# Both scores ahead of the product block in each attention step, with one third of the maximum products between them

## The chip, the cores and the metric

One Trainium2 chip, one core of it. The time is that of the device for one execution, in microseconds. The kernel before took 2652.84 us, the median of three runs (2650.61 to 2661.35).

## What is computed

The reference is one pre-norm transformer layer in fp32 on x of shape (2, 2048, 512): a causal attention with 16 heads of 32, and a feed-forward part with 8 experts of which each token uses 2, plus a shared one. The part that matters here:

```
scores = einsum('bhqd,bhkd->bhqk', q, k) / sqrt(32)
scores = where(causal, scores, -inf)
attn   = softmax(scores, axis=-1)
out    = einsum('bhqk,bhkd->bhqd', attn, v)
```

So each score is exponentiated less the maximum of its row, the row's sum divides at the end, and keys behind the query are masked.

## The kernel before

The phases follow one another: projections, attention, output projection with the shared expert, routing, experts, combination. Only `phase_attention` (L507 to L982) is touched.

Its unit of work is one group of 4 heads (8 groups over the two batches) and one chunk of 512 queries, q = 0 to 3, so 32 units. A unit goes through its key tiles of 128 keys in the order of `ORDER[q]`; the tiles from 4q on lie on the diagonal and need the mask. Each tile makes two steps, p = 0 and p = 1 (two heads each), 640 steps in all, and since every unit has an even number of steps p = 0 is an even step and p = 1 an odd one.

The row maxima of a unit are found one unit or so ahead, by a second, transposed product of q and k: a stream of 1280 "max" items and one "turn" per unit. `attention_plan` (L420) deals this stream out to the steps, `upto`, by costs that it gives the items and the room it sees in each step: mostly 3 items in odd steps, 0 to 2 in even ones. `item_shares` (L540) cuts the items of a step in three: with one item it falls into the last third, with two into the last two, with three one goes into each.

In a step, TensorE does:

- `score(n, 0)` and `score(n, 1)` (L907, the matmul at L918), each into the next of three banks `b_st` (NST = 3), so each waits for the exponential of the third score before it (L913). The second score of step n waits for the first exponential of step n-1.
- `item(i)` (L880): a maximum product (L897) into the next of three banks `b_mx`, which waits until VectorE has read the bank used three items before (L885); or the turn, four transposes (L904) of a finished unit's maxima.
- in odd steps `values` (L921), eight recorded matmuls for the two steps that lie 3 and 2 back; in even steps `count_ones` (L936), the row sums of the tile two back, if that tile is not in `POOL_TILES` (those tiles GpSimd adds up, L657, and `finish` adds them at a unit's end).

VectorE reads each maximum product (L781, on the diagonal L778) and masks the two scores of a diagonal step in their banks with one instruction (L802) or two (L806), waiting for the second score (L799). ScalarE makes the two exponentials of a step (L840) out of the banks into one of eight buffers `b_pt`; in a masked step both wait for the mask (L837). A turn's rows are copied by ScalarE (L846) ahead of the exponentials of the step whose items hold the turn (L865 to L868), and SyncE then moves them into `b_q`. All orders are written out; nothing is rearranged at run time.

The tables that place the tiles and the row sums:

```
ORDER = ((0, 1, 2, 3), (0, 1, 4, 2, 5, 3, 6, 7), (0, 1, 2, 8, 3, 4, 9, 5, 6, 10, 7, 11),
         (0, 1, 2, 12, 3, 4, 5, 13, 6, 7, 8, 14, 9, 10, 11, 15))
ONES_TILES = ((0, 1, 2, 3), (2, 6, 7), (2, 9, 6, 10, 11), (2, 4, 13, 8, 14, 15))
```

Of the kernel before, what the change touches and what calls it, by code (L numbers as in the profile page):

```python
# [46 lines left out]
def f32(ap):  # L47

    return ap.bitcast(F32)
# [457 lines left out]
def phase_attention(nc, x, w, scratch, ahead):  # L507
# [32 lines left out]
    def item_shares(n):  # L540

        here, there = upto[n - 1] if n else start, upto[n]
        return [here + (there - here) * k // 3 for k in range(4)]
# [20 lines left out]
    def key_slot(it, j):  # L564

        return (NQ * it + j) % KRING

    def unit_ending(n, offset):

        for u in range(NU):  # L570
            if first_step[u + 1] + (offset[units[u][1]] if isinstance(offset, tuple) else offset) == n:
                return u
        return None

    with ExitStack() as ctx:
# [52 lines left out]
        with nc.Block() as block:  # L628
# [140 lines left out]
            @block.vector  # L769
            def _(v):  # L770
                def partial_max(i):
                    _, u, t, h, c = stream[i]
                    q = units[u][1]
                    w = min(CH, (TPC * q + t + 1) * P - c * CH)
                    v.wait_ge(s_item, i + 1)
                    part = mpart[u % 2][:, t, h, c:c + 1]
                    if c == q:
                        v.tensor_tensor_reduce(unread[i % NMX][:, 0:w], mxb[i % NMX][:, 0:w], later[:, CH - w:], 1.0, -3e38,  # L778
                                               ALU.add, ALU.max, part).then_inc(s_red, 1)
                    else:  # L780
                        v.tensor_reduce(part, mxb[i % NMX][:, 0:w], AX.X, ALU.max).then_inc(s_red, 1)  # L781
                    if (t, h, c) == (TPC - 1, HG - 1, q):
                        v.wait_ge(s_red, maxes_before[i + 1])
                        v.tensor_reduce(mt[u % 2][:, :, 0:MROW + 1:DH], mpart[u % 2][:, :, :, 0:q + 1],
                                        AX.X, ALU.max, negate=True).then_inc(s_mcol, 1)

                v.memset(f32(kb[MROW:MROW + 1]), 1.0).then_inc(s_set, 1)
                for n in range(2):
                    v.memset(mt[n][:], 0.0).then_inc(s_set, 1)  # L789
                v.wait_ge(s_set, NSET)  # L790
                v.wait_ge(s_cst, NCST)
                for i in range(start):
                    if stream[i][0] == "max":
                        partial_max(i)
                def mask(n):
                    u, q, kt, p = steps[n]
                    d = kt - TPC * q
                    b0 = 2 * n % NST
                    v.wait_ge(s_st, 2 * n + 2)  # L799
                    if b0 + 1 < NST:  # L800
                        block = stb[:, b0:b0 + 2, d * P:(d + 1) * P]
                        v.tensor_tensor(block, block, sooner[:].unsqueeze(1).to_broadcast([P, 2, P]), ALU.add).then_inc(s_msk, 1)  # L802
                    else:
                        for b in (b0, 0):
                            block = stb[:, b, d * P:(d + 1) * P]
                            ins = v.tensor_tensor(block, block, sooner[:], ALU.add)  # L806
                        ins.then_inc(s_msk, 1)

                for n in range(NS):
                    here, _, some, there = item_shares(n)  # L810
                    for i in range(here, some):
                        if stream[i][0] == "max":
                            partial_max(i)
                    if steps[n][2] >= TPC * steps[n][1]:
                        mask(n)
                    for i in range(some, there):
                        if stream[i][0] == "max":
                            partial_max(i)
                    if n == first_step[NQ * NG - 2]:
                        v.wait_ge(s_sum, 16)  # L820
                        v.reciprocal(rsum[:], sums[:]).then_inc(s_rec, 1)
# [57 lines left out]
            def _(pe):  # L879
                def item(i):  # L880
                    what = stream[i]
                    bank = mxb[i % NMX]
                    if i >= NMX:
                        if stream[i - NMX][0] == "max":
                            pe.wait_ge(s_red, maxes_before[i - NMX + 1])  # L885
                        else:
                            pe.wait_ge(s_turn, stream[i - NMX][1] + 1)
                    if what[0] == "max":
                        _, u, t, h, c = what
                        it, q = units[u]  # L890
                        w = min(CH, (TPC * q + t + 1) * P - c * CH)
                        if (t, h, c) == (0, 0, 0):
                            pe.wait_ge(s_q[q], 48 * (it + 1))
                        if (t, h) == (0, 0) and c == q:
                            pe.wait_ge(s_k[c][it % 2], 48 * (it // 2 + 1))
                        at = key_slot(it, c) * CH
                        ins = pe.matmul(bank[:, 0:max(w, 2 * P)], qb[0:KR, h, q * CH + t * P:q * CH + (t + 1) * P],  # L897
                                        kb[0:KR, h, at:at + max(w, 2 * P)], start=True, stop=True)
                        ins.then_inc(s_item, 1)
                    else:  # L900
                        u = what[1]
                        pe.wait_ge(s_mcol, u + 1)
                        for t in range(TPC):
                            ins = pe.transpose(bank[0:MROW + 1, t * P:(t + 1) * P], mt[u % 2][:, t, :], ident[:])  # L904
                        ins.then_inc(s_item, 1)

                def score(n, j):  # L907
                    u, q, kt, p = steps[n]
                    it = units[u][0]
                    d = kt - TPC * q  # L910
                    lo = min(max(d, 0) * P, 2 * P)
                    if 2 * n + j >= NST:
                        pe.wait_ge(s_exp, 2 * n + j - NST + 1)  # L913
                    if n == first_step[u] and j == 0:
                        pe.wait_ge(s_row[q], 16 * (it + 1))
                    at = key_slot(it, kt // TPC) * CH + kt % TPC * P
                    h = 2 * p + j
                    pe.matmul(stb[:, (2 * n + j) % NST, lo:], kb[:, h, at:at + P],  # L918
                              qb[:, h, q * CH + lo:(q + 1) * CH], start=True, stop=True).then_inc(s_st, 1)
# [16 lines left out]
                def count_ones(m):  # L936
                    u, q, kt, _ = steps[2 * m]
                    if kt in POOL_TILES[q]:
                        return
                    lo = max(kt - TPC * q, 0) * P  # L940
                    begin = ONES_TILES[q][0]
                    if kt == begin and u:
                        pe.wait_ge(s_sev, u)
                    for h in range(HG):
                        ins = pe.matmul(sb[h * DH:(h + 1) * DH, lo:], ones[:],  # L945
                                        pt[(2 * m + h // 2) % NPB][:, h % 2, lo:],
                                        start=(kt == begin), stop=(kt == ORDER[q][-1] and not POOL_TILES[q]))
                    ins.then_inc(s_one, 1)
# [13 lines left out]
                for n in range(NS):  # L962
                    here, *some = item_shares(n)
                    score(n, 0)
                    for i in range(here, some[0]):
                        item(i)
                    if n % 2 == 0 and n >= 4:
                        count_ones((n - 4) // 2)
                    if n % 2 and n >= 3:
                        values((n - 3) // 2)  # L970
                    for i in range(some[0], some[1]):
                        item(i)
                    score(n, 1)
                    for i in range(some[1], some[2]):
                        item(i)
                    done = unit_ending(n, FINISH)
                    if done is not None and done in summed:
                        finish(done)
# [940 lines left out]
```

## Time and profile before

| | |
|---|---|
| median of three runs | 2652.84 us |
| profiled execution, its own time | 2644.25 us |
| its span | 2642.6 us |
| TensorE busy | 2319.7 us, 88% |
| VectorE busy | 1559.6 us, 59% |
| ScalarE busy | 1045.4 us, 40% |
| GpSimd busy | 1002.3 us, 38% |

PE is TensorE's matmuls and PEld its weight loads, which overlap them; DVE is VectorE, ACT ScalarE, POOL GpSimd. Matmuls are pipelined: a row's length is that of one matmul from start to end, and the next can start before it ends. Idle time in brackets is that of the engine just before the row, with what released it.

### The profile page before, as it was taken

What the parts mean: (1) busy time and instruction counts of PE and PEld (TensorE: products, weight loads), DVE (VectorE), ACT (ScalarE), POOL (GpSimd) and SP (SyncE); (2) the same over time, 40 slices, a digit from 0 to 9 for tenths busy, and PEclk for the clock granted to TensorE, in tenths of its full rate; (3) what the DMA queues carried; (4) which work ended last, traced back from release to release, by engine and by line L of the source; (5) the groups of instructions that cost most, each with busy time, mean ns of one, the idle gap of its engine ahead of it and who ended that gap; (6) DMA issues with size and microseconds to landing.
All of it is one profiled execution on the core that took longest, in us unless ns stands there. A gap on an engine that the chain in (4) does not pass through costs nothing. (4 is left out here: it accounts for less than half of the span.)

```text
span 2642.6 us, 34529 instructions
## 1 busy us (share of the span) xinstructions
PE 2319.7 (88%) x12088; PEld 1469.9 (56%) x12088; DVE 1559.6 (59%) x3219; ACT 1045.4 (40%) x1928; POOL 1002.3 (38%) x592
## 2 busy tenths in 40 slices
PE   5996699999999999999999599998499999999940
PEld 5775344444444444444443377776477777777730
DVE  3664686767777767767673444443645545555535
ACT  2332155555555555555556412121033333333300
POOL 0000055575655566665657613130221212111036
PEclk8998599999999999999999799999599999999975
DMA  3766511313131403323210234331245454545349
GB/s 114 272 243 224 113 33 49 81 35 93 36 81 33 97 24 93 82 57 73 49 51 23 70 114 143 113 126 50 85 146 175 144 179 139 180 136 174 96 172 368
DMA packets 178740, 301.72 MB, mean 114 GB/s; under 512 B 23616, under 2 KB 65728, under 8 KB 178624
## 3 DMA queue, kind: packets, MB, share of 16 engines
q1 hardware_dynamic: 159360, 242.54, 30.3%
q0 software_dynamic: 14656, 49.29, 6.0%
q10 hardware_dynamic: 4608, 8.39, 0.8%
q8 instruction: 66, 1.08, 0.2%
q14 instruction: 50, 0.41, 0.1%
HBM read 199.65 MB, written 100.27 MB: 113 GB/s over the span
## 5 line engine op out<-in xcount | busy, mean ns | idle before, releaser
L840 ACT ACTIVATE b_pt<-b_st 128x512 f32<-128x512 f32 (+3 forms) x1280 | 612.6, 535 | 484.4 <-DVE b_st L802 205.4
L657 POOL TENSOR_TENSOR b_acc<-b_acc,b_pt 128x1024 f32<-128x1024 f32 (+1 forms) x256 | 593.0, 2346 | 214.1 <-ACT b_pt L840 213.7
L781 DVE TENSOR_REDUCE b_mpart<-b_mx 128x1 f32<-128x512 f32 x768 | 512.2, 686 | 195.6 <-PE b_mx L897 193.0
L918 PE MATMUL b_st<-b_q,b_k 97*128 97x512 f32 (+2 forms) x1280 | 495.1, 400 | 74.2 <-ACT b_pt L840 54.7
L897 PE MATMUL b_mx<-b_k,b_q 96*128 96x512 f32 (+2 forms) x1280 | 506.6, 411 | 29.9 <-DVE b_mt L789 25.9
L897 PEld LDWEIGHTS b_mx<-b_k,b_q 96*128 96x128 f32 x1280 | 247.0, 194 | 284.9 <-DVE b_mpart L781 154.0
L918 PEld LDWEIGHTS b_st<-b_q,b_k 97*128 97x128 f32 x1280 | 241.0, 190 | 279.3 <-ACT b_pt L840 240.6
L931 PE MATMUL b_ob<-b_pt,b_v 128*32 128x512 f32 (+3 forms) x2560 | 303.0, 545 | 1.1 <-ACT b_pt L840 1.1
L778 DVE CUSTOM_DVE_ANT_0 b_unread<-b_mx,b_later 128x384 bf16<-128x384 f32 (+3 forms) x512 | 245.0, 485 | 87.7 <-PE b_mx L897 87.3
L657 POOL TENSOR_TENSOR b_acc<-b_pt 128x1024 f32<-128x1024 f32 x48 | 113.4, 2378 | 294.7 <-ACT b_pt L840 294.7
L61 PE MATMUL e_fb<-e_xh,e_w_guh 128*128 128x512 f32 (+1 forms) x552 | 219.6, 398 | 1.5 <-DVE e_xl L1738 1.5
L63 PE MATMUL e_fb<-e_xl,e_w_guh 128*128 128x512 f32 (+1 forms) x552 | 217.6, 394 | 0.0
L62 PE MATMUL e_fb<-e_xh,e_w_gul 128*128 128x512 f32 (+1 forms) x552 | 217.3, 394 | 0.0
L1710 ACT ACTIVATE e_sg<-e_fb 128x512 f32<-128x512 f32 (+1 forms) x69 | 41.2, 596 | 341.0 <-PE e_fb L63 341.0
L1682 POOL COPY e_idx<-token 128x4 uint32 (+1 forms) x23 | 4.3, 186 | 410.5 <-PE e_tb L1772 410.5
L1743 DVE TENSOR_TENSOR e_hf<-e_sg,e_fb 128x512 f32<-128x512 f32 (+1 forms) x69 | 47.4, 686 | 189.0 <-ACT e_sg L1710 189.0
L1685 POOL DMA_INDIRECT e_xg<-scr_xn,e_idx x92 | 100.2, 1090 | 39.8 <-issue 21.0
L63 PEld LDWEIGHTS e_fb<-e_xl,e_w_guh 128*128 128x128 f32 (+1 forms) x552 | 98.8, 179 | 29.5
L61 PEld LDWEIGHTS e_fb<-e_xh,e_w_guh 128*128 128x128 f32 (+1 forms) x552 | 98.9, 179 | 29.1 <-issue 1.8
L945 PE MATMUL b_sb<-b_pt,b_ones 128*32 128x512 f32 (+3 forms) x1152 | 115.0, 471 | 0.0
L62 PEld LDWEIGHTS e_fb<-e_xh,e_w_gul 128*128 128x128 f32 (+1 forms) x552 | 98.8, 179 | 27.8
L802 DVE TENSOR_TENSOR b_st<-b_st,b_sooner 128x256 f32<-128x256 f32 x171 | 73.2, 428 | 67.0 <-PE b_st L918 66.8
(224 smaller groups left out, 3517.4 us busy)
## 6 DMA issues: line engine op xcount, KB each, us to landing
scr_y<-e_y SPq DMA_DIRECT2D x23, 1024.0 KB, 5.1
b_q<-scr_qh SPq DMA_DIRECT2D x64, 256.0 KB, 4.4
b_k<-scr_kh SPq DMA_DIRECT2D x64, 256.0 KB, 4.0
e_gu<-in_L_ffn_w_gate_dram SPq DMA_DIRECT2D x23, 704.0 KB, 5.7
e_gu<-in_L_ffn_w_up_dram SPq DMA_DIRECT2D x23, 704.0 KB, 7.2
e_d<-in_L_ffn_w_down_dram SPq DMA_DIRECT2D x23, 512.0 KB, 7.4
a_xin<-in_L_attn_x_dram POOLq DMA_DIRECT2D x8, 1024.0 KB, 6.0
scr_qh<-a_qh SPq DMA_DIRECT2D x8, 1024.0 KB, 4.6
```

Of the source, the lines that this page charges most:

```text
L61: nc.tensor.matmul(out, wh, xh, start=first, stop=False)
L62: nc.tensor.matmul(out, wl, xh, start=False, stop=False)
L63: return nc.tensor.matmul(out, wh, xl, start=False, stop=last)
L657: g.tensor_tensor(out[:, :, lo:], so_far[:, :, lo:], pt[n % NPB][:, :, lo:], ALU.add).then_inc(s_add, 1)
L778: v.tensor_tensor_reduce(unread[i % NMX][:, 0:w], mxb[i % NMX][:, 0:w], later[:, CH - w:], 1.0, -3e38, ALU.add, ALU.max, part).then_inc(s_ ...
L781: v.tensor_reduce(part, mxb[i % NMX][:, 0:w], AX.X, ALU.max).then_inc(s_red, 1)
L840: act.activation(pt[n % NPB][:, j, lo:], stb[:, (2 * n + j) % NST, lo:], ACT.Exp, scale=SCALE).then_inc(s_exp, 1)
L897: ins = pe.matmul(bank[:, 0:max(w, 2 * P)], qb[0:KR, h, q * CH + t * P:q * CH + (t + 1) * P], kb[0:KR, h, at:at + max(w, 2 * P)], start=Tr ...
L918: pe.matmul(stb[:, (2 * n + j) % NST, lo:], kb[:, h, at:at + P], qb[:, h, q * CH + lo:(q + 1) * CH], start=True, stop=True).then_inc(s_st, 1)
L931: ins = pe.matmul(ob[h * DH:(h + 1) * DH, lo:], vbuf[:, kt, h * DH:(h + 1) * DH], pt[(2 * m + h // 2) % NPB][:, h % 2, lo:], start=(kt == ...
L945: ins = pe.matmul(sb[h * DH:(h + 1) * DH, lo:], ones[:], pt[(2 * m + h // 2) % NPB][:, h % 2, lo:], start=(kt == begin), stop=(kt == ORDER ...
L1685: g.indirect_dma_start(out=xg[n][:, t, :], in_=scratch["xn"], out_offset=None, in_offset=bass.IndirectOffsetOnAxis(ap=idx[n][:, t:t + 1], ...
```

## The change

Three edits. On TensorE the second score moves ahead of the ones or value block and ahead of the second third of the items:

```
                     score(n, 0)
                     for i in range(here, some[0]):
                         item(i)
+                    score(n, 1)
+                    for i in range(some[0], some[1]):
+                        item(i)
                     if n % 2 == 0 and n >= 4:
                         count_ones((n - 4) // 2)
                     if n % 2 and n >= 3:
                         values((n - 3) // 2)
-                    for i in range(some[0], some[1]):
-                        item(i)
-                    score(n, 1)
                     for i in range(some[1], some[2]):
                         item(i)
```

On VectorE the mask of a step comes behind the first third of the step's maxima in place of two thirds, so that its order agrees with TensorE's:

```
                 for n in range(NS):
-                    here, _, some, there = item_shares(n)
+                    here, some, _, there = item_shares(n)
                     for i in range(here, some):
```

Plan, counts of instructions, buffers and all other queues stay.

## Rows read from the trace of the kernel before

**Rows 1.** The page: busy us, share, instructions; granted clock in 40 slices.

```profile
PE 2319.7 (88%) x12088; PEld 1469.9 (56%) x12088; DVE 1559.6 (59%) x3219; ACT 1045.4 (40%) x1928; POOL 1002.3 (38%) x592
...
PEclk8998599999999999999999799999599999999975
```

**Rows 2.** Stretch, us, busy us (instructions) PE, PEld, DVE, ACT, POOL; clock, DMA, GB/s.

```profile
330.00:1470.00 1140.00, 1077.89 (x6458) 495.53 (x6454) 783.77 (x2051) 649.33 (x1360) 702.21 (x303) 1.00 0.23 57
```

**Rows 3.** Waits in 330 to 1470 us: total, times, longest.

```profile
PEld b_st L918 <- ACT b_pt L840: 239.7, 375, 1.9
...
DVE b_mpart L781 <- PE b_mx L897: 171.2, 234, 1.8
...
PE b_st L918 <- ACT b_pt L840: 54.5, 108, 1.5
```

**Rows 4.** Timeline, 679.8 to 681.8 us: start us, us, engine, line, operation.

```profile
679.79 0.44 PE L918 MATMUL b_st<-b_q,b_k 97*128 97x384 f32 x1
...
680.07 0.40 PE L897 MATMUL b_mx<-b_k,b_q 96*128 96x512 f32 x1
...
680.31 0.39 PE L918 MATMUL b_st<-b_q,b_k 97*128 97x512 f32 x1
680.33 0.42 DVE L802 TENSOR_TENSOR b_st<-b_st,b_sooner 128x256 f32<-128x256 f32 x1
680.66 0.68 DVE L781 TENSOR_REDUCE b_mpart<-b_mx 128x1 f32<-128x512 f32 x1
680.87 1.36 ACT L840 ACTIVATE b_pt<-b_st 128x384 f32<-128x384 f32 x3 [0.76 <-DVE b_st L802]
681.41 0.19 PEld L918 LDWEIGHTS b_st<-b_q,b_k 97*128 97x128 f32 x1 [1.06 <-ACT b_pt L840]
681.42 0.50 PE L918 MATMUL b_st<-b_q,b_k 97*128 97x512 f32 x1 [0.72 <-ACT b_pt L840]
...
681.76 0.40 PE L897 MATMUL b_mx<-b_k,b_q 96*128 96x512 f32 x1
```

**Rows 5.** Timeline, 599.0 to 601.1 us, where a ones block follows.

```profile
598.99 0.39 PE L918 MATMUL b_st<-b_q,b_k 97*128 97x256 f32 x1 [0.38 <-ACT b_pt L840]
...
599.41 0.50 DVE L806 TENSOR_TENSOR b_st<-b_st,b_sooner 128x128 f32<-128x128 f32 x2 [0.65 <-PE b_st L918]
599.77 1.07 PE L945 MATMUL b_sb<-b_pt,b_ones 128*32 128x512 f32 x8
...
601.10 0.40 PE L918 MATMUL b_st<-b_q,b_k 97*128 97x512 f32 x1
```

**Rows 6.** Timeline, 544.6 to 546.5 us, a turn in an odd step.

```profile
544.60 0.68 PE L904 MATMUL b_mx<-b_ident,b_mt 128*97 128x128 f32 x4
...
545.31 0.60 ACT L846 ACTIVATE b_rows<-b_mx 97x512 fp32r<-97x512 f32 x1 [2.38 <-PE b_mx L904]
...
546.45 0.39 PE L918 MATMUL b_st<-b_q,b_k 97*128 97x256 f32 x1 [0.94 <-ACT b_pt L840]
```

**Rows 7.** Timeline, 632.3 to 634.7 us, a turn in an even step.

```profile
632.33 0.60 PE L904 MATMUL b_mx<-b_ident,b_mt 128*97 128x128 f32 x4
...
632.96 0.60 ACT L846 ACTIVATE b_rows<-b_mx 97x512 fp32r<-97x512 f32 x1 [0.50 <-PE b_mx L904]
...
633.32 1.06 PE L931 MATMUL b_ob<-b_pt,b_v 128*32 128x512 f32 x8
...
634.65 0.40 PE L918 MATMUL b_st<-b_q,b_k 97*128 97x512 f32 x1
```

**Rows 8.** Exponentials by shape, 330 to 1470 us: busy, mean ns, idle before.

```profile
L840 ACT ACTIVATE b_pt<-b_st 128x512 f32<-128x512 f32 x892 | 491.2, 601 | 244.0 <-PE b_st L918 169.2 <-DVE b_st L802 43.0 <-DVE b_st L806 22.4
...
L840 ACT ACTIVATE b_pt<-b_st 128x128 f32<-128x128 f32 x127 | 28.5, 275 | 60.5 <-DVE b_st L802 37.7 <-DVE b_st L806 22.8
```

**Rows 9.** Busy time and clock around one fall of the clock.

```profile
970.00:978.00 8.00, 7.06 (x46) 3.60 (x38) 5.21 (x19) 3.95 (x8) 5.73 (x3) 1.00 0.01 3
978.00:982.00 4.00, 4.00 (x20) 1.59 (x22) 1.96 (x9) 0.74 (x3) 0.00 (x0) 0.57 0.01 2
```

More of the change, by code:

```diff
@@ L966, in _ @@
                         item(i)
+                    score(n, 1)
+                    for i in range(some[0], some[1]):
+                        item(i)
                     if n % 2 == 0 and n >= 4:
@@ L970, in _ @@
                         values((n - 3) // 2)
-                    for i in range(some[0], some[1]):
-                        item(i)
-                    score(n, 1)
                     for i in range(some[1], some[2]):
```

## The prediction

> **What bounds the kernel now.** I read the page's busy shares and its clock row first [rows 1]. TensorE is busy 88% of the span, the next engine 59%, and the clock row stands at 9 (over 90%) from the sixth slice of 66 us to the 23rd, the attention stage, the only one the diff touches; 330 to 1470 us lies inside it. In that stretch [rows 2] TensorE is busy 1077.89 of 1140.00 us, VectorE 783.77, ScalarE 649.33, GpSimd 702.21, at a granted clock of 1.00. So TensorE's queue sets the time there, and what it waits for is a straight loss. The others have a quarter to two fifths to spare.
>
> What it waits for stands in the waits [rows 3]: scores (L918) for an exponential (L840), 54.5 us in 108 waits, and in the queue's own view 239.7 us in 375. Neither figure is the loss. A 512-column matmul is shown 0.40 us long, but the next one starts 0.24 us after it (680.07 to 680.31 in [rows 4]), so the first view misses some 0.16 us of each wait, and the second counts time in which the array was streaming. The honest measure is the distance between starts, less 0.24.
>
> Two stalls can be seen. In [rows 4] the second score of a step (a diagonal tile, so with a mask) starts at 679.79. The mask follows at 680.33 (0.42 long), the exponentials at 680.87, and the next step's second score, which needs the bank that the first of them frees, starts at 681.42: 1.63 us after 679.79. In between TensorE had only a maximum product and a score to issue (680.07, 680.31), so it stood for 681.42 - 680.31 - 0.24 = 0.87 us. In [rows 5] the same chain runs from 598.99 (mask at 599.41), but the next step has a ones block in it (599.77, 1.07 us) and a maximum product, and the second score goes at 601.10 with no wait named. So the rule of this stage is: **from the second score of a masked step to the second score of the next, TensorE needs about 1.6 us of other work; one 1.07 us block in that interval is enough, and scores and maxima alone are not.**
>
> **The change, part by part.** It adds and removes no instruction. Every step still has two scores, its maximum products in thirds, and one value block (odd steps) or one ones block (even steps whose tile two back is summed by TensorE). Only places change: the block moves from before the second score to behind it, and VectorE's mask from behind two thirds of the maxima to behind one third. SyncE, GpSimd and ScalarE keep their order.
>
> (A) *Which intervals hold a block.* Call the two steps of a tile even and odd. Before, the interval odd to even holds the block of the even step, the ones block of the tile one back in ORDER, if it is in ONES_TILES; even to odd always holds a value block. After, odd to even always holds the value block of the odd step, and even to odd holds the ones block that the even step issues, that of the tile two back. Counted for the masked tiles of one group of heads from the two tables: before, without a block: none for q=0, tiles 4 and 6 for q=1, tiles 9 and 11 for q=2, tiles 13 and 15 for q=3, 6 of 16. After: tile 0 of q=0, all four of q=1, tiles 8, 9, 10 of q=2, tiles 12, 14, 15 of q=3, 11 of 16. The uncovered one at q=0 has three or four maximum products in its step and its interval comes to about 1.4 us, so I price it at 0.25. That leaves 10 against 6, over 8 groups 32 uncovered intervals more. In the new ones TensorE has a score, a maximum product, a score and a maximum product; diagonal scores are narrow, and four such starts come to 0.65 to 0.8 us, about what the old ones hold (679.79 to 680.31 and 0.24 more is 0.76). So the price is that of [rows 4], 0.87 us. A score that comes out of a wait is also slower: its successor starts 0.34 later (681.42 to 681.76) and not 0.24, 0.10 more. 32 x 0.97 = 31 us, and 8 x 0.25 = 2: **+33 us**. Bounds: in the best case the mask starts 0.42 after its score [rows 5], is 0.42 long, and a narrow exponential ends by 1.3, a price of 0.6 at all 80; in the worst VectorE is a maximum behind, 1.1 at all 80 and 0.8 at the eight. Against 48 x 0.87 = 42 of now, that is +6 to +52. I take the middle row because it is the same chain with the same number of maxima around it.
>
> On that 0.10 the Trainium skill, "TensorE: Matmul & The Clock Gate", section "Architectural detail: the array is 16× 32×32, not 1× 128×128", says that the engine can pull a weight load ahead of matmuls in flight. By that the load of a waiting score would be over when its wait ends, and the term would be 3 us less. The rows speak against it here: the load starts at 681.41 and the matmul at 681.42, since the wait sits on the load.
>
> (B) *The turn of the row maxima.* ScalarE copies the transposed maxima (L846) ahead of the step's exponentials. In [rows 6], an odd step with the turn last, the transposes start at 544.60, the copy at 545.31 (0.60 long, with two exponentials behind it), and the next step's second score at 546.45, 1.85 us after the transposes and 0.94 us of it idle. Nothing covers this before or after; where one of that step's maxima leaves the interval it grows by 0.24, eight times at most, 2 us. [rows 7] is the even kind: transposes 632.33, copy 632.96, value block 633.32, and the second score long after, with no wait. With the change that score comes before the value block: 0.43 for the transposes and two starts of 0.24 stand against 1.85, a wait of 0.94. Even steps carry the turn last in 6 groups, and one odd one (step 17) loses a ones block: 7 x 0.94. **+9 us** together, between +2 and +12.
>
> (C) *What gets shorter.* The first score of the step behind a stall of [rows 4] waits a little for the second exponential of the masked step; after, a value block or the stall itself covers it. That one ends 0.28 to 0.60 us behind the first [rows 8], and TensorE has 0.28 + 0.24 to issue meanwhile (679.79, 680.07, 680.31 in [rows 4]), so 0 to 0.2 us each with the hand-over; at the 48 stalls and about as many near ones 0.1 us is **-10 us** (0 to -15).
>
> (D) *Mask earlier, maxima.* In a step with three maxima the mask stands behind one and not two, which shortens its wait by up to 0.69 us, but there a value block covers the chain anyway, so it is worth nothing on the path. Each new stall lets VectorE catch up, and a few waits of L897 for it go: **-6 us** (0 to -15). The maxima, values and ones are themselves not late: a value block needs exponentials of the step before last and a ones block older ones, and both come later than before; eight buffers b_pt keep their reuse 3 to 4 steps away. If that cover were gone ScalarE would wait on L834, which costs TensorE only beyond its own 490 us of slack.
>
> Sum +33 +9 -10 -6 = +26 us on the profiled execution (span 2642.6, its own time 2644.25), so 2670 for a run like it. The median shown is 8.6 us above it, and what is reported is a median: 2652.84 + 26 = **2679 us**.
>
> **Rivals.**
> *Faster:* the odd-to-even stalls vanish (48 x 0.87 = 42 us) and the new even-to-odd ones are cheap, because in an even step the mask stands behind no maximum and VectorE, idle 171 us for L897 in this stretch [rows 3], is caught up. At 0.6 us each 48 us come back; with the full 15 + 15 of (C) and (D) and only 2 of (B) it is 48 + 2 + 2 - 42 - 30 = -20, 2633 us. It decides where the price of an uncovered interval falls below some 0.5 us at all 80. For it: 599.41 is only 0.42 behind its score. Against: the odd step before ends with a maximum behind its value block, TensorE starts one every 0.24 us where VectorE needs 0.68 (at 680.66 in [rows 4]).
> *No change:* stalls on TensorE are partly exchanged, since a stall lets the others catch up and shortens the next; half of (A) and all of (C), (D): +16 + 9 - 10 - 6 = +9, 2662 us, or with less of (B) within the bound.
> *The clock:* in 978 to 982 us the granted clock was 0.57, so the lower of its two levels for most of it, after 8 us in which TensorE was busy 7.06 [rows 9]. With stalls closer together this could come in each unit. One such fall costs about 1.7 us (3.4 us at half speed), 16 of them 27 us, so 2679 + 27 = 2706 us; the stretch has at least 108 waits of scores and a mean clock of 1.00, which is against it. The Trainium skill, "TensorE: Matmul & The Clock Gate", section "A second HAM failure mode: psum-queue depth-cycling", has this mechanism: short idles between groups of matmuls while banks are cycled make the clock drop and return.
>
> **How the numbers follow.** Forecast 0.56, the clock 0.13, no change 0.20, faster 0.08, something else 0.03. This kernel's measurement tells about 0.5% (13 us) from nothing. Slower by more than that: the forecast except its lowest end, the clock, and a little of the exchange case: 0.72. Within: 0.19. Faster: 0.09. The range is 2654 to 2712: below, (A) near its low bound with (B); above, (A) at its high bound with (B), or the clock's case. The rest of the no-change case and the faster case are left out.
>
> **What would show it.** The profile after should have more waits of L918 for L840 by some 25 to 40, the first view of [rows 3] at 80 to 100 us; the second score of odd steps in q=1 units standing 0.9 us behind the first, and that of even steps following a value block without a wait; the attention stage some 26 us longer, the stages around it unchanged; counts of all groups the same. It is wrong if the uncovered intervals show mask starts 0.42 behind their score and waits under 0.6, if the stage gets shorter, or if the clock row in the stage changes.

## The result, and the profile after

The changed kernel takes 2697.42 us, the median of four runs, against 2651.73 us: a ratio of 1.0163, 95% interval 1.0119 to 1.0207. It is slower by 46 us, where 26 were forecast; the time lies in the range. Its profiled execution has a span of 2696.9 us against 2642.6, 54 us more, and 51 of them lie in the attention stage (from the first score to the last output copy 1223.1 us, before 1171.8). That the medians are only 46 us apart has a reason in the clock: the profiled execution of the kernel before is one of its shortest (2644.25 us, mean granted clock 0.941). Seventeen later executions of it took 2643 to 2661 us, and the longer ones are those with the lower mean clock, down to 0.933. Counts of instructions are the same.

The stretch of the stage again, as [rows 2] (stretch, its us, busy us with instructions of PE, PEld, DVE, ACT and POOL, granted clock, DMA share, GB/s):

```profile
330.00:1470.00 1140.00, 1051.93 (x6170) 482.61 (x6169) 789.65 (x2042) 612.04 (x1286) 658.45 (x284) 0.98 0.22 56
```

In the same time TensorE gets 288 fewer matmuls done (6170 against 6458), and the clock is 0.98 and not 1.00. The waits of that stretch, as [rows 3]:

```profile
PE b_st L918 <- ACT b_pt L840: 82.8, 111, 1.3
```

The sum rises from 54.5 to 82.8 us, the number hardly (108 to 111, where 25 to 40 more were forecast): many short waits went, long ones came. One of them, an open interval of the changed order, from a q=1 unit (timeline, columns as in [rows 4]):

```profile
655.36 0.51 PE L918 MATMUL b_st<-b_q,b_k 97*128 97x384 f32 x2
...
655.71 0.39 PE L897 MATMUL b_mx<-b_k,b_q 96*128 96x512 f32 x1
...
655.95 0.33 PE L918 MATMUL b_st<-b_q,b_k 97*128 97x384 f32 x1
656.17 0.42 DVE L802 TENSOR_TENSOR b_st<-b_st,b_sooner 128x256 f32<-128x256 f32 x1
656.50 0.68 DVE L781 TENSOR_REDUCE b_mpart<-b_mx 128x1 f32<-128x512 f32 x1
656.71 0.87 ACT L840 ACTIVATE b_pt<-b_st 128x384 f32<-128x384 f32 x2 [2.00 <-DVE b_st L802]
657.25 0.19 PEld L918 LDWEIGHTS b_st<-b_q,b_k 97*128 97x128 f32 x1 [1.34 <-ACT b_pt L840]
657.25 0.44 PE L918 MATMUL b_st<-b_q,b_k 97*128 97x384 f32 x1 [0.97 <-ACT b_pt L840]
657.36 0.19 PEld L897 LDWEIGHTS b_mx<-b_k,b_q 96*128 96x128 f32 x1
657.53 0.40 PE L897 MATMUL b_mx<-b_k,b_q 96*128 96x512 f32 x1
```

Both scores of the even step start together at 655.36 (the second 0.18 later), then one maximum product and the odd step's first score; the mask comes at 656.17, the exponentials at 656.71, the odd step's second score only at 657.25. It could have started at 656.12, 0.17 behind the score before: a stall of 1.13 us. VectorE's mask starts 0.63 us behind its score, because a maximum is still being reduced.

The even kind of turn, priced from [rows 7] without having been seen:

```profile
644.62 0.60 ACT L846 ACTIVATE b_rows<-b_mx 97x512 fp32r<-97x512 f32 x1 [1.12 <-PE b_mx L904]
644.66 0.40 PE L897 MATMUL b_mx<-b_k,b_q 96*128 96x512 f32 x1
...
645.12 1.08 ACT L840 ACTIVATE b_pt<-b_st 128x512 f32<-128x512 f32 x2
...
645.76 0.19 PEld L918 LDWEIGHTS b_st<-b_q,b_k 97*128 97x128 f32 x1 [1.14 <-ACT b_pt L840]
645.76 0.50 PE L918 MATMUL b_st<-b_q,b_k 97*128 97x512 f32 x1 [0.70 <-ACT b_pt L840]
```

645.76 - 644.66 - 0.24 = 0.86 us, where 0.94 was forecast.

The cleanest measure is a whole group of heads, 80 steps from one output copy of a q=3 unit to that of the next, since groups repeat each other. Three in a row of the kernel before:

```profile
474.14:617.84 143.70, 136.54 (x826) 63.64 (x824) 102.14 (x270) 82.05 (x174) 88.29 (x38) 1.00 0.25 60
617.84:761.56 143.72, 136.57 (x826) 63.69 (x824) 102.22 (x272) 82.13 (x173) 88.23 (x38) 1.00 0.25 60
761.56:905.35 143.79, 136.49 (x826) 63.65 (x824) 102.31 (x273) 82.13 (x173) 88.25 (x38) 1.00 0.24 60
```

and the same three of the changed kernel:

```profile
481.17:629.28 148.11, 137.14 (x826) 63.45 (x824) 103.20 (x270) 81.77 (x173) 88.16 (x38) 1.00 0.23 58
629.28:779.12 149.84, 138.52 (x825) 63.81 (x824) 103.38 (x272) 81.77 (x174) 88.13 (x38) 0.99 0.23 57
779.12:931.87 152.75, 141.64 (x826) 64.57 (x825) 103.64 (x273) 81.89 (x174) 88.18 (x38) 0.97 0.23 57
```

The first column after the stretch is its length. Two different losses can be told apart. Where the clock stays at 1.00 the group takes 148.11 us, 4.4 more than before: that is the order. Where it falls, the same work takes 1.7 and 4.6 us more again. Behind the first 25 us of the stage, which run at the lower level in both kernels, the clock is at its lower level for 47.6 us and before for 10.2; half of the difference, 19 us, is lost. Of the stage's 51 us that leaves some 33 for the order. Group by group, with half of the time at the lower level taken off, it is 3.2 to 4.9 us, 33 in all eight.

Between the medians the clock has a smaller part. The four executions of the changed kernel have a mean clock of 0.933 to 0.936 over the whole program, so about 357 us at the lower level, and the seventeen of the kernel before about 335; half of the difference is 11 us, and 33 + 11 = 44 of the 46.

### The profile page after: what moved, and what is told of

Read it like the earlier page. It is cut to its first block and busy times, and to the rows that moved or that the text cites. A ratio compares the mean times of both kernels' runs of the same rounds, so it can differ in the third digit from the quotient of the medians.

```text
span 2696.9 us, 34529 instructions
## 1 busy us (share of the span) xinstructions
PE 2343.2 (87%) x12088; PEld 1475.2 (55%) x12088; DVE 1568.0 (58%) x3219; ACT 1043.2 (39%) x1928; POOL 1004.2 (37%) x592
## 5 line engine op out<-in xcount | busy, mean ns | idle before, releaser
L897 PE MATMUL b_mx<-b_k,b_q 96*128 96x512 f32 (+2 forms) x1280 | 522.0, 425 | 30.4 <-DVE b_mt L789 25.9
L918 PE MATMUL b_st<-b_q,b_k 97*128 97x512 f32 (+2 forms) x1280 | 455.7, 396 | 105.5 <-ACT b_pt L840 87.7
```

## The experiments

All times beside 2646 to 2653 us for the kernel before, which was measured again beside each batch of runs (2651.73 us with the changed kernel; 2646.20 with its mask late, with its stalls filled and with the two kernels without a mask; 2649.08 with the halves and the two unfilled orders per step; 2652.73 with the last two), so a difference between rows of two batches can be off by up to 6 us; "group" is the length of the group of heads that starts first after 465 us, as above.

| kernel | open of 16 | median us | group us | clock in it |
|---|---|---|---|---|
| before | 6 | 2651.73 | 143.70 | 1.00 |
| changed | 11 | 2697.42 | 148.11 | 1.00 |
| changed, mask late | 11 | 2783.49 | 161.87 | 0.94 |
| changed, stalls filled | 11 | 2679.58 | 148.10 | 1.00 |
| before, no mask | - | 2577.95 | 134.89 | 1.00 |
| changed, no mask | - | 2600.51 | 137.34 | 1.00 |
| odd steps only | 16 | 2772.05 | 157.45 | 0.97 |
| even steps only | 16 | 2745.31 | 157.52 | 0.97 |
| order per step | 4 | 2640.25 | 141.96 | 1.00 |
| the same, other ones tiles | 3 | 2639.48 | 141.79 | 1.00 |
| order per step, stalls filled | 4 | 2626.46 | 141.94 | 1.00 |
| before, stalls filled | 6 | 2644.61 | 143.66 | 1.00 |

**The mask late.** In the changed kernel, VectorE alone goes back:

```
-                    here, some, _, there = item_shares(n)
+                    here, _, some, there = item_shares(n)
```

> The order of TensorE is that of the changed kernel; only VectorE's mask goes back behind two thirds of the step's maxima. Theory (waits behind masked steps, opened by the places of the blocks): in odd steps the mask now stands behind a second maximum, 0.69 us of VectorE, and the value block behind it has only some 0.3 us to spare, so at about 90 odd-to-even intervals 0.1 to 0.3 us come back as waits: 10 to 25 us slower than the changed kernel, 2707 to 2722 us. Rival (the loss of the change lies in VectorE's new order, a maximum held up behind an early mask): undoing it gives back most of the 46 us, 2655 to 2670 us.

Measured: 2783.49 us, 86 slower than the changed kernel. The direction was the theory's, the size was not: the rival is dead, but 10 to 25 us was far too little. The profiled execution is the longer of the two, 104 us above that of the changed kernel (2802.17 against 2698.58), all of it in the stage. In it the clock is at its lower level for 177 us of the stage, 130 more than in the changed kernel, which is 65 of the 104 us. The other 39 are the order: the maximum that the mask now stands behind is issued *after* the second score. By the distances of starts in the first group, six of the open intervals (tile 0 in q=0, 6, 9 and 10, 12 and 14) stall 0.35 to 0.7 us longer and the others as long as in the changed kernel, and intervals that hold a value block now stall 0.3 to 0.6 us. So the edit on VectorE was not the harmful part of the change: without it the loss would have been nearly three times as large.

**The stalls filled.** The changed kernel repeats the first score of an odd masked step 3 to 6 times (3, 4, 6, 6 by the tile's place on the diagonal) where the interval is open. Only the last repeat counts for the semaphore, and both exponentials wait for the mask anyway:

```
+                    for r in range(fill(n)):
+                        score(n, 0, r + 1)
                     score(n, 1)
```

> The changed kernel with 3 to 6 extra repeats of the first score of an odd masked step, some 0.7 us of matmuls, where TensorE stands for about 1 us anyway because no block lies in the interval (88 places); the results are the same. Theory: the repeats hide in the stalls and cost nothing, units without a fall of the clock keep their time (q=1 at 29.2 us, q=3 at 57.2). Clock theory (12 us or more of the loss are falls of the granted clock that follow the stalls): the falls go and the kernel gets 10 to 18 us faster than the changed one, about 2683 us. Rival (the array is not really free there, the time is lost elsewhere): 88 x 0.7 = 60 us slower, 2757 us; without any clock effect 2697 us.

Measured: 2679.58 us, 18 faster than without (12 if each is set beside its own measurement of the kernel before; 18 between the profiled executions). The same three groups:

```profile
483.00:631.10 148.10, 144.37 (x876) 70.61 (x874) 103.26 (x270) 81.80 (x173) 88.26 (x38) 1.00 0.24 58
631.10:779.28 148.18, 144.12 (x876) 70.56 (x874) 103.39 (x272) 81.79 (x173) 88.27 (x38) 1.00 0.23 59
779.28:927.54 148.26, 144.28 (x876) 70.58 (x874) 103.57 (x273) 81.91 (x174) 88.32 (x38) 1.00 0.23 58
```

TensorE does 50 matmuls more in each and takes not 0.01 us longer than the undisturbed group of the changed kernel (148.10 against 148.11). So the array really stood idle there, and the gain is the clock: 6.8 us at the lower level in the stage in place of 47.6, half the difference is 20, and the stage is 16 us shorter. The other executions agree: the four with the repeats have a mean clock of 0.940 to 0.942, the four without 0.933 to 0.936. The Trainium skill, "TensorE: Matmul & The Clock Gate", section "A second HAM failure mode: psum-queue depth-cycling", tells of a kernel in which short idles between groups of matmuls make the clock drop and return; this pair agrees.

**No mask.** The kernel before and the changed one, without the causal mask of the diagonal tiles: the instruction and the waits for it are left out, and the exponentials of those tiles have a scale 1024 times smaller.

```
-                        if kt >= TPC * q:
-                            act.wait_ge(s_msk, masked(n) + 1)
-                        else:
-                            act.wait_ge(s_st, 2 * n + j + 1)
+                        act.wait_ge(s_st, 2 * n + j + 1)
```

> The kernel before without its causal mask on the diagonal tiles (left out: the 341 instructions of VectorE and the waits for them; the exponentials of diagonal tiles get a small scale so that they stay finite). Theory: the chain behind masked steps loses its 0.43 us instruction and its wait for both scores, so the stalls there go, 50 to 75 us: 2580 to 2600 us. Rival (the stalls are the exponentials' own): less than 20 us faster.

> The same left out of the changed kernel. Theory: the two orders now differ only by the waits at the turns, 5 to 15 us slower than the kernel before without its mask. Rival (the order itself costs, by the maxima, the values or the turns): the difference stays at 30 us or more.

Measured: 2577.95 and 2600.51 us. The mask costs the kernel before 68 us (its group takes 134.89 and not 143.70 us), which lies 2 us beyond the range given; the run takes the instruction's time on VectorE away together with the waits, and does not tell the two apart. Of the difference between the orders 23 us are left and 2.45 us a group, above the 5 to 15 us expected. So the masked steps carry 2 of the 4.4 us of a group; the rest is there without them. By the distances of starts in one group, 0.9 us of it is the turn of the even kind, 0.2 the other turn, 1.3 are waits of 0.1 to 0.3 us of second scores where an interval is open, 0.3 are like ones in two intervals of unmasked steps, and 0.5 are waits ahead of maxima; against them 0.5 us of waits of first scores went. The theory of the mask alone was too narrow by 8 us.

**One half alone.** Only odd steps (shown), or only even steps, take the new order, on TensorE and VectorE:

```
+                    if n % 2:
+                        score(n, 1)
+                        for i in range(some[0], some[1]):
+                            item(i)
...
```

> Only in odd steps does the second score come ahead of the value block (with the mask behind one third there); even steps are as before. Theory: from the second score of an even masked step to that of the odd one there is now no block at all, 16 of 16 intervals of a group of heads open, from odd to even both blocks, none open. Against the changed kernel (11 open) 5 x 8 more waits of about 0.95 us, 38 us, and some 10 us of falls of the clock: 2745 us (2730 to 2765). Rival (the loss of the change comes from the ones blocks moving in even steps): no slower than the changed kernel, 2650 to 2697 us.

> Only in even steps does the second score come ahead of the ones block; odd steps are as before. Theory: from odd to even no block, 16 of 16 open, from even to odd both, none open. Against the kernel before (6 open) 80 more waits of about 0.85 us less what they spare elsewhere, some 60 us, and falls of the clock, 15 us: 2725 us (2700 to 2750). Rival (the loss of the change comes from the value block moving in odd steps): 2650 to 2665 us.

Measured: 2772.05 and 2745.31 us. Each half alone is worse than both, as the count of open intervals says: in the full change the block of one kind of step moves into the interval that the other kind's block leaves. The first is 7 us above its range, the second within. The first group of each takes 157.45 and 157.52 us, both at a clock of 0.97 (10.2 us at the lower level, so 5.1 lost), so 16 open intervals cost the same from either side. Over the stage the clock is at its lower level for 133 and 88 us, and the half of that difference, 22 us, is most of the 27 us between the two.

**The order per step.** The kernel before, with the new order only in the two steps of tile 11 (q=2) and of tile 13 (q=3), and the value block last in an odd step that ends with a turn (`ones_in(n)` is true where step n holds a ones block, `turn_last(n)` where the turn is in the last third of its items):

```
+    def scores_first(n):
+        even = n - n % 2
+        diagonal = steps[n][2] >= TPC * steps[n][1] > 0
+        return diagonal and ones_in(even) and not ones_in(even + 2)
+    def block_last(n):
+        return n % 2 == 1 and n in turn_step.values() and turn_last(n) and not ones_in(n + 1)
```

> The kernel before, but the order of the change only in the two steps of tile 11 in q=2 units and tile 13 in q=3 units, where both intervals then hold a block (4 of 16 open in place of 6), and the value block at the very end of an odd step whose last item is a turn (8 places), between the turn and the next scores. Theory: 16 waits of 0.62 and 1.15 us go (14 us) and 8 of 1.10 us (9 us): 23 us faster than the kernel before, ratio 0.991 (0.988 to 0.995). Rival (a wait removed only moves to the next maximum or exponential): no difference.

> The last one, and in q=2 units TensorE sums the rows of tile 4 in place of tile 9, so that the ones block of tile 4 fills the interval behind tile 9 (3 of 16 open). Theory: 8 waits of 0.92 us go, a full block in place of a narrower one costs 0.2 us each: 5 us less than the last one, ratio 0.989 (0.985 to 0.994); the plan deals its maxima out a little differently (109 of 640 steps), which makes this one less sure. Rival (GpSimd, which takes tile 9 late in the unit, holds up its end): slower than the last one.

Measured: 2640.25 us, ratio 0.9967 (0.9953 to 0.9981), a third of what was expected. Its groups:

```profile
477.23:619.19 141.96, 136.78 (x826) 63.95 (x824) 101.96 (x270) 82.16 (x174) 88.20 (x38) 1.00 0.24 60
619.19:761.02 141.83, 136.67 (x826) 64.07 (x824) 102.09 (x272) 82.17 (x173) 88.25 (x38) 1.00 0.25 61
761.02:904.75 143.73, 138.29 (x826) 64.15 (x824) 102.20 (x273) 82.36 (x173) 88.19 (x38) 0.99 0.24 60
```

The three stalls of a group went to nothing (by the starts of the scores 1.10, 0.61 and 1.16 us, 2.9 together), and others came further down, one of 0.5 us ahead of a maximum behind the moved turn, one of 0.3 at the second score of tile 11, and small ones: 1.8 us a group are won where the clock stays up, 15 us in all. But the clock is at its lower level for 30.6 us of the stage, 20 more than before, which takes 10 of them back. The version with other ones tiles is the same within the measurement (2639.48 us, ratio 0.996, 0.9947 to 0.9974; expected 5 us less).

**The same with its stalls filled**, and the kernel before with its own filled. The repeats are now those of an even step's first score behind an odd masked one:

```
+                    if n % 2 or not n or steps[n - 1][2] < TPC * steps[n - 1][1] or ones_in(n) or scores_first(n - 1):
+                        return 0
+                    return (3, 4, 6, 6)[max(steps[n][2] - TPC * steps[n][1], 0)]
```

> The kernel with the order chosen per step, and in its open odd-to-even intervals 3 to 6 repeats of the even step's first score, some 0.7 us of matmuls in waits of about 0.9 us; the results are the same. Theory: the repeats hide, a group of heads takes as long as without them where the clock stays up, and the falls of the clock in the attention stage (30.6 us there at the lower level) mostly go, worth some 10 us: about 2630 us, ratio to the kernel before 0.993 (0.990 to 0.996). Rival (falls have nothing to do with the waits): no change from 0.9967, or slower by what the repeats cost.

> The same repeats in the kernel before. Theory: its attention stage had only 10.2 us at the lower level, so there is at most 5 us to get back: ratio 0.998 to 1.001. Rival (the repeats themselves speed something up, as by an engine kept awake): as much as in the other pair, 0.4% or more.

Measured: 2626.46 us, ratio 0.9909 (0.9885 to 0.9933), the fastest of all, 26 us under the kernel before, by 0.9% better than it and 2.6% better than the change:

```profile
471.13:613.07 141.94, 139.08 (x841) 66.32 (x839) 101.99 (x270) 82.16 (x174) 88.36 (x38) 1.00 0.25 60
613.07:754.87 141.80, 138.97 (x841) 66.39 (x839) 102.11 (x272) 82.15 (x174) 88.33 (x38) 1.00 0.25 61
754.87:896.99 142.12, 139.07 (x841) 66.31 (x839) 102.16 (x273) 82.21 (x173) 88.31 (x38) 1.00 0.25 60
```

15 matmuls more a group, the same length, and only 3.4 us at the lower level in the whole stage. The kernel before with the same repeats takes 2644.61 us, ratio 0.9974 (0.9958 to 0.9989), a little more gain than expected; its profiled stage is as long as without them (1171.9 us), as that execution of the kernel before was one with few falls to begin with. The other executions show where the 0.3% come from: the seventeen of the kernel before have a mean clock of 0.933 to 0.941 (0.937 on average), the twelve with its stalls filled 0.938 to 0.942 (0.940). That is 17 us less at the lower level, so 8 us, which is the difference of the medians. The same reckoning for the order per step gives 0.933 to 0.935 without and 0.938 to 0.942 with the repeats, 34 us less at the lower level and 17 us gained; each beside its own kernel before, the two medians are 17 us apart.

## Why the prediction was right in kind and short in size

- *What bounds the stage, and the rule of the open interval* held for the open ones. Group times rise and fall with the number of open intervals: 4, 6, 11 and 16 of them go with 141.9, 143.7, 148.1 and 157.5 us (the last with 5.1 us of clock in it, so 152.4 without; the first is also rid of a turn's stall of 1.10 us). From 6 to 11 and from 11 to 16 an interval more costs 0.88 and 0.86 us, near the 0.87 of [rows 4]. The stalls stand where the tables put them: by the starts of the scores behind tiles 4, 5, 6, 7 in q=1, 8, 9, 10 in q=2 and 12, 14, 15 in q=3, and not one of the ten is missing. Those from odd to even are gone, but for 0.48 us behind tile 0 in q=0.
- *(A), +33 us, came out at some 24, from larger terms on both sides.* The ten new open intervals stall 0.96 us on average in the group of 148.11 us (0.58 to 1.19) and not 0.87, as an interval holds narrower scores and VectorE is behind by a maximum. But the rule that one block in the interval is enough was wrong, and its own row showed it: the score at 598.99 in [rows 5] has waited 0.38 us for an exponential, although its interval holds a value block of 1.06 us:

```profile
597.54 1.06 PE L931 MATMUL b_ob<-b_pt,b_v 128*32 128x512 f32 x8
...
598.99 0.39 PE L918 MATMUL b_st<-b_q,b_k 97*128 97x256 f32 x1 [0.38 <-ACT b_pt L840]
```

Four such intervals lost 0.15 to 0.45 us each in the kernel before. In q=0 the block is only 0.43 us long (kernel before, too):

```profile
470.24 0.43 PE L897 MATMUL b_mx<-b_k,b_q 96*128 96x512 f32 x1
...
470.60 0.43 PE L931 MATMUL b_ob<-b_pt,b_v 128*32 128x128 f32 x8
...
470.96 0.50 PE L897 MATMUL b_mx<-b_k,b_q 96*128 96x512 f32 x1
...
471.82 0.50 PE L918 MATMUL b_st<-b_q,b_k 97*128 97x512 f32 x1 [0.36 <-ACT b_pt L840]
```

So the interval of tile 0 in q=0, priced at 0.25 as new, stalls 0.81 us after and had stalled 0.63 before. The intervals that the change closes gave back more than six prices too: 4.6 us a group by the six open ones, and 1.6 more by those that had held a ones block and stalled 0.2 to 0.5 us all the same.
- *The whole sum.* Taking from each distance of two starts about the shortest one of the same pair of instructions leaves this, in us of one group (143.70 and 148.11 us):

| stall ahead of | before | after |
|---|---|---|
| second scores of odd steps, masked step before | 1.8 | 10.8 |
| second scores of even steps, masked step before | 6.7 | 0.6 |
| second scores behind an unmasked step, with the turns | 1.6 | 2.7 |
| first scores | 0.9 | 0.6 |
| maxima | 4.1 | 4.3 |
| the ones and value blocks, in and around them | 22.4 | 22.9 |

The first two rows are (A): 3 us a group, 24 in eight. The last row is mostly the blocks' own fixed cost; only its difference counts.
- *(B), +9,* was right: 0.86 us at the even turn where 0.94 was forecast, and at the odd one 1.30 in place of 1.10, together 1.1 us a group and 9 in all, at the places named.
- *(C), -10, and (D), -6, are the terms that failed.* The waits of first scores fell by 0.3 to 0.4 us a group, 3 us in all: in the kernel before they came to 0.9 us a group, so there was less to win than (C) takes away. The waits ahead of maxima did not fall at all (4.1 and 4.3 us), so (D) came out at +2 and not at -6: that a stall lets VectorE catch up and saves such waits is not what the runs show. Some 4 us at the blocks had no term. So the order costs 33 to 36 us against 26, and that the sum was as near as that is partly luck, since (A) was too large by 9 where (C) and (D) were too good by 15. That 46 us lie in the range although the sum is 20 short is due to its upper half, which was drawn from (A) at its high bound and from the clock's case: 7 to 10 of the 20 are the order's, some 11 the clock's.
- *The mask on VectorE, (D), costed at nothing on the path,* was right as the changed kernel has it, and the cover that the text named (a value block) is thin: one maximum more ahead of the mask cost 86 us, 65 of 104 in the profiled pair by the clock.
- *The clock* had been a rival with 0.13 and 27 us. It is not a rival but a part of the same case: 19 us came on top of the order in the profiled pair, about 11 between the medians, and the sum had it at nothing. The prediction named a change of the clock in the stage as a sign of being wrong; by [rows 2] it went from 1.00 to 0.98. The argument against it, 108 waits and a mean clock of 1.00 in [rows 3] and [rows 2], looked at their number. What changed was their length and how close they stand. Of the ten falls four come behind tile 10 in q=2, where a turn's stall of 1.30 us and an open interval's of 0.64 end 1.5 us apart (705.23 and 706.71, the fall at 707), and three where a group begins; one comes behind the four stalls of 0.7 to 1.2 us of a q=1 unit, two in the last group. The groups from 481.17 and from 931.87 have the same stalls and no fall, so what decides a single fall is not shown.
- *The term of 0.10 us for the matmul behind a stalled score* held: the next one starts 0.28 us later (657.25 to 657.53) where an unstalled one takes 0.17. Load and matmul both start at 657.25, so a weight load pulled ahead (the Trainium skill, "TensorE: Matmul & The Clock Gate", section "Architectural detail: the array is 16× 32×32, not 1× 128×128") again doesn't show at a stalled score.

## What to carry to other kernels

With a ring of three banks between TensorE, VectorE and ScalarE, ask of every long chain (here mask and exponential, 1.6 us) which work TensorE has between its start and the score that needs the bank, and lay the one long block there; moving it fills one interval by emptying its neighbour, so decide place by place and not for all steps. Don't take an interval for covered because a block lies in it: read the distance of starts there too. Count what a stall does to the clock as well: in this kernel it added a third between the medians and more than half in the profiled pair. Where a stall can't be filled with useful work, repeated matmuls that nobody waits for kept the clock up and were free.

## What was not expected of the hardware

The granted clock falls behind stalls that are each near 1 us long and stand close together, in a stage whose rows show TensorE busy nearly all the time: the group with clock 0.97 has 141.64 us busy of 152.75. Just ahead of a fall of the changed kernel it is less, 5.38 us of 7.00:

```profile
700.00:707.00 7.00, 5.38 (x35) 2.90 (x29) 4.09 (x20) 2.64 (x6) 2.31 (x1) 1.00 0.01 4
707.00:711.00 4.00, 4.00 (x21) 1.21 (x20) 1.46 (x7) 1.42 (x4) 0.00 (x0) 0.57 0.00 0
```

Filling the stalls took the lower level in the stage from 47.6 to 6.8 us, and in the last pair from 30.6 to 3.4 us. One fall of 3.4 us costs 1.73 us (149.84 against 148.11).
